# Query turning moved two projections back, router judging moved later, and one layernorm's statistics moved into the stage before it, in a one-core transformer kernel on Trainium2

## Chip, core and metric

The kernel runs on one core of a Trainium2 chip. The metric is device time in microseconds of one execution. The kernel before was timed three times: 2847.12 us in the median, 2845.57 to 2850.18. TensorE (PE in the profile) multiplies and transposes, VectorE (DVE) and ScalarE (ACT) do elementwise work and reductions, GpSimd (POOL) does elementwise work between on-chip tiles, SyncE (SP) issues transfers. Each engine works through its own queue in order and waits on semaphores that others raise.

## The reference

One sequence of 2048 tokens of width 256 goes through four residual blocks. Each begins with a layernorm.

```python
x = x + attn_a(layernorm(x), ...)   # 16 heads, low-rank keys and values, a mask of top-k index scores
x = x + ffn(layernorm(x), ...)      # 8 routed experts, 2 per token, and a shared one
x = x + attn_b(layernorm(x), ...)   # 16 heads of 16, ALiBi
x = x + ffn(layernorm(x), ...)      # the same weights again
```

The parts that the change touches:

```python
def layernorm(x): m = mean(x); v = var(x); return (x - m) / sqrt(v + 1e-5)

# attn_a: the index mask
index_scores = einsum('bhqk,h->bqk', relu(qi @ ki), idx_w)     # 2048 x 2048
thr = sorted_desc(index_scores)[adaptive_k - 1]                # one threshold per row
mask = where(index_scores >= thr, 0, -1e9), with the causal mask
# attn_a: its queries
q = (x @ Wq).reshape(b, s, 16, 128 + 64); rope on the last 64
scores = q_full @ k_full * scale + mask

# ffn: the router
scores = softmax(xf @ gate_w); sel = top_k(scores + expert_bias, 2)
out = shared(xf); out[token] += routed expert of the token
```

## The kernel before

The 2048 rows are 16 tiles of 128 (`NT`), `x` stays on chip, and `xT` holds the normalized rows transposed. Every stage is a block in which each engine has a queue written out by hand. Between blocks all engines meet at a barrier, so a block's end is its last engine's end. There is no scheduler: the order in the code is the order in the queue.

**Index threshold** (`index_threshold`, called twice, once for each half of the mask's rows; `g` is 0 or 1, `ixt0` and `ixt1` in semaphore names). VectorE and ScalarE search the k-th largest score of each row. Five probes (`PROBES`) each try a midpoint: VectorE counts the scores above it in four of eight row tiles (L784), ScalarE in the other four with a sign and a sum (L629), then VectorE narrows the bounds with some twenty small operations and publishes the next midpoint (`mid_ready`, L724), at last `hi_ready` (L806). A step over eight row tiles follows: ScalarE writes marks above `hi` (L637, L642), VectorE masks and takes the top eight (L810, L813). Then VectorE writes the mask `bias` (L730, L736). The first threshold writes the short rows of the causal triangle, the second the long ones.

Beside the search runs a second job, eight heads' queries for 16 row tiles, "pairs" `n` = 0 to 15, since each has two halves of four heads:

- TensorE projects pair `n` (L664) into two of four PSUM banks and raises `projected`.
- ScalarE copies it to `q_nat[n % 3]` (L590, `store_projected`) and raises `q_ready`.
- GpSimd applies the rope to the pair in place (L571 to L575), behind a given midpoint, and raises `roped`.
- TensorE turns the pair, eight transposes (L674), into two PSUM banks that all pairs share, once the pair before has been copied from them (`q_taken`), and raises `flipped`.
- ScalarE copies the turned pair to `q_out` (L600, `store_flipped`) and raises `q_taken`; SyncE stores it to HBM (L552).

ScalarE's order is a list of units: copies of projections 0 and 1, then alternately projection `n + 2` and turned pair `n`. Three units stand after each probe's signs, one after every second row tile of the step above `hi`, the rest at the end. TensorE's order is projection `n`, turning `n - 1`. Behind all pairs stands a small matmul (L678), for which VectorE waits with `ix_unsolved` (L834); then the block ends.

**Layernorm** (`layernorm`, four times). VectorE takes statistics of 16 tiles (`bn_stats`, L137), computes mean and variance, ScalarE the square root, VectorE normalizes tile by tile (L158), TensorE transposes (L206), ScalarE stores to `xT` (L173). The second and fourth also compute the router's logits: for each quarter `n` of the rows `judge(n)` multiplies `gate_w` by `xT` (L189), `keep_verdict(n)` on ScalarE copies the result (L167), `turn_verdict(n)` transposes it on TensorE (L197).

**Experts** (`experts`, twice). At its end VectorE adds the two routed results of each quarter of the rows to `x` (L2316, L2318), as the quarter's transfers land. The first call is followed by the third layernorm.

## Time and profile before

| what | value |
|---|---|
| median of three runs | 2847.12 us |
| the profiled execution | 2841.48 us |
| its span, first to last instruction | 2839.6 us |
| TensorE matmul busy | 2335.7 us, 82% of the span |
| VectorE busy | 1783.8 us, 63% |
| ScalarE busy | 1678.7 us, 59% |
| GpSimd busy | 704.2 us, 25% |
| mean granted TensorE clock | 0.908 |

The profile is of one execution. Its busy shares are averages over stages, and each stage here has another limit. A wait is read from the idle time before an instruction and from what released it. The first index threshold lies at 169 to 359 us, the second at 462 to 653, the four layernorms end near 24, 1784, 2007 and 2628. The granted clock of a stretch is a share of 2.4 GHz: 0.5 is the lower of TensorE's two levels, 1.2 GHz, and values between are stretches with both.

### The profile page before, as it was taken

Reading aid. Unit: us, or ns where it says so; the run is one execution under the profiler, and the core shown is the slowest. Engines: PE = TensorE matmul, PEld = TensorE weight load, DVE = VectorE, ACT = ScalarE, POOL = GpSimd, SP = SyncE. Lnnn points to the kernel's source line nnn. Section 1 sums busy time; section 2 is a strip of 40 time slices with the busy share of each in tenths; the row PEclk is TensorE's granted clock in tenths of the full one; section 3 lists DMA queues with packets and bytes.
Section 4 is the critical chain, followed back from the end, with each engine's and each line's share of the span. In section 5 each row is a group of like instructions: output and inputs, shape, how many; then the busy total and the mean of one; then the engine's idle time right before and its main releaser. Section 6 shows DMA issues by size and latency. Waiting matters only on the chain. (4 is left out here: it accounts for less than half of the span.)

```text
span 2839.6 us, 42530 instructions
## 1 busy us (share of the span) xinstructions
PE 2335.7 (82%) x12560; PEld 1566.7 (55%) x12561; DVE 1783.8 (63%) x3726; ACT 1678.7 (59%) x3051; POOL 704.2 (25%) x974
## 2 busy tenths in 40 slices
PE   4954585556999999999999997986639999997985
PEld 2532253225877787877777885554315444434653
DVE  4786669673777677767776776523347778823523
ACT  2776667673877777777777765232306777763232
POOL 0213420342422332133225322154010000000153
PEclk9977897787999999999999998998858999977998
DMA  1011101014100000000001001223360303000124
GB/s 47 0 38 45 53 22 37 37 52 136 31 16 12 21 21 15 12 24 16 16 8 31 8 1 59 77 78 115 132 99 1 46 2 46 2 1 3 53 80 135
DMA packets 78250, 115.62 MB, mean 41 GB/s; under 512 B 24658, under 2 KB 52146, under 8 KB 75058
## 3 DMA queue, kind: packets, MB, share of 16 engines
q1 hardware_dynamic: 67796, 91.62, 11.6%
q0 software_dynamic: 10240, 21.38, 2.5%
q8 instruction: 105, 1.72, 0.2%
q14 instruction: 109, 0.89, 0.1%
HBM read 70.63 MB, written 41.94 MB: 40 GB/s over the span
## 5 line engine op out<-in xcount | busy, mean ns | idle before, releaser
L1389 DVE TENSOR_TENSOR aa_pt_lo<-psum,aa_pt_hi 128x512 fp32r<-128x512 f32 x544 | 350.5, 686 | 82.6 <-ACT aa_pt_hi L1319 80.0
L1840 DVE TENSOR_REDUCE ab_part_max<-psum 128x2 f32<-128x1024 f32 (+3 forms) x320 | 327.3, 1062 | 116.4 <-PE psum L1678 114.4
L1782 ACT ACTIVATE ab_prob<-psum 128x512 f32<-128x512 f32 (+3 forms) x640 | 298.0, 542 | 121.2 <-PE psum L1707 117.1
L1319 ACT ACTIVATE aa_pt_hi<-psum 128x512 fp32r<-128x512 f32 x544 | 297.4, 598 | 116.2 <-PE psum L1249 113.3
L1376 DVE CUSTOM_DVE_ANT_0 aa_prob<-psum,bias 128x512 f32<-128x512 f32 (+2 forms) x480 | 278.7, 598 | 113.2 <-PE psum L1239 93.9
L1237 PE MATMUL psum<-ka_hi,aa_q_hi 128*128 128x512 f32 (+3 forms) x640 | 267.9, 419 | 11.1 <-POOL aa_q_lo L1171 8.3
L1203 POOL TENSOR_TENSOR x<-aa_y_out,x 128x256 f32<-128x256 f32 x256 | 188.2, 735 | 353.4 <-ACT aa_y_out L1337 308.7
L1249 PE MATMUL psum<-ident,aa_prob 128*128 128x128 f32 x1600 | 253.0, 274 | 6.8 <-issue 5.5
L1707 PE MATMUL psum<-ab_q_stack,ab_k_stack 50*128 50x512 f32 (+3 forms) x640 | 243.7, 460 | 13.2 <-ACT ab_prob L1782 8.8
L1311 ACT ACTIVATE aa_prob<-aa_prob,aa_neg_max 128x128 f32<-128x128 f32 (+11 forms) x192 | 228.0, 1188 | 43.8 <-DVE aa_neg_max L1382 42.0
L1260 PE MATMUL psum<-aa_pt_hi,c_stack 128*128 128x512 f32 x544 | 233.6, 429 | 5.9 <-ACT aa_out_t L1326 4.3
L1238 PE MATMUL psum<-ka_lo,aa_q_hi 128*128 128x512 f32 (+3 forms) x640 | 235.8, 368 | 2.0 <-issue 2.0
L1239 PE MATMUL psum<-ka_hi,aa_q_lo 128*128 128x512 f32 (+3 forms) x640 | 236.3, 369 | 0.0
L1678 PE MATMUL psum<-ab_k_stack,ab_q_stack 49*128 49x512 f32 (+3 forms) x640 | 230.4, 475 | 6.3 <-DVE ab_part_max L1840 6.0
L1262 PE MATMUL psum<-aa_pt_lo,c_stack 128*64 128x512 f32 x544 | 215.5, 396 | 0.0
L1249 PEld LDWEIGHTS psum<-ident,aa_prob 128*128 128x128 f32 x1600 | 193.7, 141 | 30.3 <-issue 8.3
L1707 PEld LDWEIGHTS psum<-ab_q_stack,ab_k_stack 50*128 50x128 f32 x640 | 119.2, 203 | 116.7 <-ACT ab_prob L1782 84.9
L674 PE MATMUL psum<-ident,ixt_q_nat 128*128 128x128 f32 x256 | 46.7, 342 | 148.6 <-ACT ixt_q_out L600 141.6
L1171 POOL TENSOR_TENSOR aa_q_lo<-aa_q_row,aa_q_hi 128x512 fp32r<-128x512 f32 x64 | 82.4, 1289 | 333.1 <-ACT aa_q_hi L1303 333.1
L1719 PE MATMUL psum<-ab_prob,values 128*17 128x512 f32 (+3 forms) x1280 | 163.2, 585 | 0.0
L664 PE MATMUL psum<-ixt_w_heads,xT 128*128 128x512 f32 x256 | 141.2, 704 | 22.4 <-ACT ixt_w_heads L583 22.4
L2161 DVE SCALAR_TENSOR_TENSOR f_h<-psum,f_found,f_silu 128x224 f32<-128x224 f32 x80 | 36.1, 451 | 188.1 <-ACT f_silu L2129 188.1
(334 smaller groups left out, 4922.8 us busy)
## 6 DMA issues: line engine op xcount, KB each, us to landing
q_rows<-ixt_q_out SPq DMA_DIRECT2D x64, 256.0 KB, 2.1
aa_q_row<-q_rows SPq DMA_DIRECT2D x64, 256.0 KB, 2.6
f_back<-done SPq DMA_DIRECT2D x16, 512.0 KB, 7.6
w<-in_w SPq DMA_DIRECT2D x6, 896.0 KB, 11.3
x<-in_hidden SPq DMA_DIRECT2D x2, 2048.0 KB, 11.5
ab_q_stack<-stash_q_hi SPq DMA_DIRECT2D x32, 128.0 KB, 10.4
ab_k_stack<-stash_k_hi SPq DMA_DIRECT2D x32, 128.0 KB, 11.9
ixt_wq_n<-in_Wq_nope_T SPq DMA_DIRECT2D x2, 1024.0 KB, 5.6
```

Source lines behind the costliest of these rows:

```text
L1237: nc.tensor.matmul(out[:, 0:w], q_hi[t % 2][:, head], k_hi[:, cols], start=True, stop=False)
L1238: nc.tensor.matmul(out[:, 0:w], q_hi[t % 2][:, head], k_lo[:, cols], start=False, stop=False)
L1239: nc.tensor.matmul(out[:, 0:w], q_lo[t % 2][:, head], k_hi[:, cols], start=False, stop=True).then_inc(scores_ready, 1)
L1249: last = nc.tensor.transpose(turn_bank[(TB[t] + j) % RING][:, h * P:(h + 1) * P], prob[t % 2][h][:, j * P:(j + 1) * P], const["ident"][:])
L1260: nc.tensor.matmul(out[:], c_stack[:, j, :], pt_hi[ring][:], start=j == 0, stop=j == t, skip_group_check=True)
L1319: nc.scalar.activation(pt_hi[(TB[t] + j) % RING][:], turn_bank[(TB[t] + j) % RING], ACT.Copy).then_inc(pt_hi_done, 1)
L1376: nc.vector.tensor_tensor_reduce(prob[t % 2][h][:, c * CH:c * CH + w], score_bank[(QB[t] + h * chunks[t] + c) % 2][:, 0:w], bias[:, TRI[t] ...
L1389: nc.vector.tensor_tensor(pt_lo[ring][:], turn_bank[(TB[t] + j) % RING], pt_hi[ring][:].bitcast(F32), ALU.subtract).then_inc(pt_lo_done, 1)
L1678: nc.tensor.matmul(out[:, 0:w], q[at, t * P:(t + 1) * P], k[at, part * CH:part * CH + w], start=not diag, stop=True, skip_group_check=True ...
L1707: nc.tensor.matmul(out[:, 0:w], k[at, kb * P:(kb + 1) * P], q[at, q0:q0 + w], start=not diag, stop=True, skip_group_check=True).then_inc(t ...
L1782: nc.scalar.activation(prob[i % 2][h][:, 0:w], t_bank[slot % RING][:, 0:w], ACT.Exp).then_inc(t_taken, 1)
L1840: nc.vector.tensor_reduce(part_max[e % 2][:, at:at + 5:4, part], s_pair[pair % 2][:, :, 0:w], AX.X, ALU.max).then_inc(s_used, 1)
```

## The change

1. On TensorE in the index threshold the turning of pair `n` stands behind projection `n + 2` instead of `n + 1`. ScalarE's and GpSimd's orders stay.
2. In the second and fourth layernorm `judge(n)` moves three transposed tiles back, from tile 4(n+1) to tile 4(n+1)+3, and `turn_verdict(n)` from there to behind `judge(n + 1)`. ScalarE's `keep_verdict(n)` moves four tiles back.
3. The first `experts` takes the third layernorm's statistics: four `bn_stats` behind each quarter's additions, into a tile `stats` that `program` now allocates. The third layernorm gets them and leaves its own out.

```diff
-                    if logits is not None and t >= 5 and t % 4 == 1:
-                        keep_verdict(t // 4 - 1)
+                    if logits is not None and t >= 9 and t % 4 == 1:
+                        keep_verdict(t // 4 - 2)
                 if logits is not None:
+                    keep_verdict(NCH - 2)
                     keep_verdict(NCH - 1)
...
-                    if logits is not None and t >= 4 and t % 4 == 0:
+                    if logits is not None and t >= 7 and t % 4 == 3:
                         judge(t // 4 - 1)
-                    if logits is not None and t >= 4 and t % 4 == 3:
-                        turn_verdict(t // 4 - 1)
+                        if t >= 11:
+                            turn_verdict(t // 4 - 2)
                 if logits is not None:
                     judge(NCH - 1)
+                    turn_verdict(NCH - 2)
                     turn_verdict(NCH - 1)
...
-                for n in range(PAIRS + 1):
+                for n in range(PAIRS + 2):
...
-                    if n >= 1:
-                        pe.wait_ge(roped, n)
-                        if n >= 2:
-                            pe.wait_ge(q_taken, 2 * (n - 1))
+                    if n >= 2:
+                        pe.wait_ge(roped, n - 1)
+                        if n >= 3:
+                            pe.wait_ge(q_taken, 2 * (n - 2))
                         for i in range(2):
                             for h in range(GH):
                                 last = nc.tensor.transpose(flip_bank[i][:, h * P:(h + 1) * P],
-                                                           q_nat[(n - 1) % RING][:, i * GH + h, :], const["ident"][:])
+                                                           q_nat[(n - 2) % RING][:, i * GH + h, :], const["ident"][:])
...
                     nc.vector.tensor_tensor(here, here, back[n][1][:], ALU.add).then_inc(added, 1)
+                    if stats is not None:
+                        dve.wait_ge(added, n + 1)
+                        for t in range(n * CHUNK, (n + 1) * CHUNK):
+                            nc.vector.bn_stats(stats[:, t, :], x[:, t, :])
...
+        stats = sb("stats", [P, NT, 6])
...
-            experts(nc, "f1", x, xT, xn, bank, const, router, w13, w2, shared_in, routed_in, rows, done)
-        layernorm(nc, "ln3", x, xT, bank, const["ident"], mean, rstd)
+            experts(nc, "f1", x, xT, xn, bank, const, router, w13, w2, shared_in, routed_in, rows, done, stats=stats)
+        layernorm(nc, "ln3", x, xT, bank, const["ident"], mean, rstd, stats=stats)
```

TensorE's queue in the first index threshold, before, from the turning of pair 0 on (`ixt_q_nat_1375` to `_1377` are the three tiles of the ring, `ixt_w_heads` the projection's weights):

```order
L674 MATMUL psum<-ident,ixt_q_nat_1375 128x128 [waits ixt0_roped]
L674 MATMUL psum<-ident,ixt_q_nat_1375 128x128 x7
L664 MATMUL psum<-ixt_w_heads,xT 128x512 [waits ixt0_q_ready]
L664 MATMUL psum<-ixt_w_heads,xT 128x512 x3
L674 MATMUL psum<-ident,ixt_q_nat_1376 128x128 [waits ixt0_q_taken,ixt0_roped]
L674 MATMUL psum<-ident,ixt_q_nat_1376 128x128 x7
L664 MATMUL psum<-ixt_w_heads,xT 128x512 [waits ixt0_q_ready]
L664 MATMUL psum<-ixt_w_heads,xT 128x512 x3
```

The same place of the changed kernel, from projection 2 on:

```order
L669 MATMUL psum<-ixt_w_heads,xT 128x512 [waits ixt0_q_ready]
L669 MATMUL psum<-ixt_w_heads,xT 128x512 x3
L679 MATMUL psum<-ident,ixt_q_nat_1375 128x128 [waits ixt0_roped]
L679 MATMUL psum<-ident,ixt_q_nat_1375 128x128 x7
L669 MATMUL psum<-ixt_w_heads,xT 128x512 [waits ixt0_q_ready]
L669 MATMUL psum<-ixt_w_heads,xT 128x512 x3
L679 MATMUL psum<-ident,ixt_q_nat_1376 128x128 [waits ixt0_q_taken,ixt0_roped]
L679 MATMUL psum<-ident,ixt_q_nat_1376 128x128 x7
```

Projection 3, the second of the projections in either piece, stood behind the turning of pair 1 with its wait for `q_taken`, and now stands ahead of it.

TensorE's queue in the second layernorm, before (`xn_first` are normalized tiles, two transposes each; `f_gate_w` is a judgement, `ln_verdict` a verdict's turning):

```order
L206 MATMUL psum<-ident,xn_first 128x128 x10
L189 MATMUL psum<-xT,f_gate_w 8x512 x2
L206 MATMUL psum<-ident,xn_first 128x128 x6
L197 MATMUL psum<-ident,ln_verdict 128x8 x4
L206 MATMUL psum<-ident,xn_first 128x128 x2
```

And now:

```order
L210 MATMUL psum<-ident,xn_first 128x128 x16
L193 MATMUL psum<-xT,f_gate_w 8x512 x2
L210 MATMUL psum<-ident,xn_first 128x128 x8
L193 MATMUL psum<-xT,f_gate_w 8x512 x2
L201 MATMUL psum<-ident,ln_verdict 128x8 x4
```

The first verdict's turning stood three tiles behind its judgement, and now stands four tiles and the next judgement behind it.

VectorE's queue at the end of the first experts, now, for one quarter (`f_back` are the routed results; before, the additions of the quarters stood next to each other):

```order
L2321 TENSOR_TENSOR x<-x,f_back 128x1024 [waits ln1_stats_done]
L2323 TENSOR_TENSOR x<-x,f_back 128x1024 [waits ixs0_staged]
L2327 BN_STATS stats<-x 128x6 [waits ixs0_cleared]
L2327 BN_STATS stats<-x 128x6 x3
L2321 TENSOR_TENSOR x<-x,f_back 128x1024 [waits ixp_dve_step]
```

Four of the sixteen statistics lie between the additions of two quarters. (Semaphores are reused by later stages under their first name.)

## Rows read from the trace of the kernel before

**Rows 1.** Waits, first threshold: engine line, waited for: us, times, longest

```profile
PE psum L674 <- ACT ixt_q_out L600: 70.8, 14, 10.6
ACT ixt_q_nat L590 <- PE psum L664: 55.4, 22, 5.6
```

**Rows 2.** Waits, second index threshold

```profile
ACT ixt_q_nat L590 <- PE psum L664: 56.1, 22, 5.6
```

**Rows 3.** Timeline, ScalarE: start, us, engine line op [idle before]

```profile
211.90 1.06 ACT L590 ACTIVATE ixt_q_nat<-psum 128x512 f32<-128x512 f32 x2
...
219.22 0.60 ACT L590 ACTIVATE ixt_q_nat<-psum 128x512 f32<-128x512 f32 x1 [5.29 <-PE psum L664]
...
221.38 1.99 ACT L629 ACTIVATE x<-ix_scores,ix_neg_mid 128x2048 bf16<-128x2048 f32 x1
...
229.75 1.06 ACT L600 ACTIVATE ixt_q_out<-psum 128x512 f32<-128x512 f32 x2
...
292.38 1.99 ACT L637 ACTIVATE x<-ix_scores,ix_neg_hi 128x2048 bf16<-128x2048 f32 x1
```

**Rows 4.** Timeline, TensorE, after the first probe's signs

```profile
214.08 1.94 PE L674 MATMUL psum<-ident,ixt_q_nat 128*128 128x128 f32 x8 [5.18 <-ACT ixt_q_out L600]
215.81 5.03 PE L664 MATMUL psum<-ixt_w_heads,xT 128*128 128x512 f32 x8
```

**Rows 5.** Timeline, VectorE, first to second probe

```profile
212.03 0.17 DVE L787 TENSOR_SCALAR ix_count<-ix_signs 128x4 f32<-128x4 f32 x1 [5.66 <-ACT x L629]
...
215.34 2.35 DVE L784 TENSOR_SCALAR_CACHE_REDUCE bias<-ix_scores,ix_mid 128x2048 bf16<-128x2048 f32 x1 [0.38 <-DVE ix_neg_mid L724]
```

**Rows 6.** Windows (us, PE/PEld/DVE/ACT/POOL busy, PEclk, DMA, GB/s); timelines, tail

```profile
214.00:231.00 17.00, 6.81 (x17) 3.76 (x18) 10.92 (x21) 10.43 (x12) 7.79 (x8) 0.70 0.08 31
328.00:359.00 31.00, 20.28 (x82) 11.06 (x82) 18.88 (x31) 11.93 (x23) 22.62 (x20) 0.99 0.26 101
...
335.72 1.07 PE L674 MATMUL psum<-ident,ixt_q_nat 128*128 128x128 f32 x8 [1.76 <-ACT ixt_q_out L600]
336.62 3.60 PE L664 MATMUL psum<-ixt_w_heads,xT 128*128 128x512 f32 x8
...
357.47 1.09 PE L674 MATMUL psum<-ident,ixt_q_nat 128*128 128x128 f32 x8 [1.91 <-POOL ixt_q_nat L575]
...
344.51 1.60 POOL L575 TENSOR_TENSOR ixt_q_nat<-ixt_straight,ixt_crossed 128x512 f32<-128x512 f32 x1
...
353.45 1.26 POOL L571 TENSOR_TENSOR ixt_straight<-ixt_q_nat,ixt_rope 128x512 f32<-128x512 f32 x1 [2.28 <-ACT ixt_q_nat L590]
```

**Rows 7.** Timelines, ScalarE and VectorE, end of the first threshold

```profile
327.28 1.06 ACT L590 ACTIVATE ixt_q_nat<-psum 128x512 f32<-128x512 f32 x2
...
345.02 2.12 DVE L736 TENSOR_TENSOR bias<-bias,causal 128x128 bf16<-128x128 bf16 x8
358.79 0.16 DVE L834 TENSOR_SCALAR ix_unsolved<-psum 128x1 int32<-128x1 f32 x1 [11.65 <-PE psum L678]
```

**Rows 8.** Timelines, ScalarE and VectorE, end of the second threshold

```profile
620.81 1.06 ACT L590 ACTIVATE ixt_q_nat<-psum 128x512 f32<-128x512 f32 x2
...
633.03 12.25 DVE L730 TENSOR_SCALAR bias<-ix_scores,ix_thr 128x1152 bf16<-128x1152 f32 x8
645.31 4.81 DVE L736 TENSOR_TENSOR bias<-bias,causal 128x128 bf16<-128x128 bf16 x8
653.06 0.16 DVE L834 TENSOR_SCALAR ix_unsolved<-psum 128x1 int32<-128x1 f32 x1 [2.93 <-PE psum L678]
```

**Rows 9.** Waits and timeline, TensorE, second layernorm

```profile
PE psum L197 <- ACT ln_verdict L167: 2.2, 4, 0.7
...
1784.09 0.41 PE L197 MATMUL psum<-ident,ln_verdict 8*128 8x8 f32 x4 [0.68 <-ACT ln_verdict L167]
```

**Rows 10.** Timeline, VectorE, first experts' end and third layernorm

```profile
1981.42 1.23 DVE L2316 TENSOR_TENSOR x<-x,f_back 128x1024 f32<-128x1024 f32 x1 [0.53 <-DMA f_back<-done]
...
1993.27 5.32 DVE L137 BATCH_NORM_STATS2 ln_stats<-x  x16 [3.44 <-PEq L91]
```

More of the change, by code:

```diff
@@ L96, in __exit__, with layernorm @@
         return super().__exit__(kind, *rest)
-def layernorm(nc, tag, x, xT, bank, ident, mean, rstd, keep=None, gate_w=None, gate_in=None, logits=None, load=None):
+def layernorm(nc, tag, x, xT, bank, ident, mean, rstd, keep=None, gate_w=None, gate_in=None, logits=None, load=None, stats=None):
     DEEP = 4
@@ L103, in layernorm @@
         sb, sem = phase.sb, phase.sem
-        stats = sb("stats", [P, NT, 6])
+        known = stats is not None
+        if not known:
+            stats = sb("stats", [P, NT, 6])
         half = sb("half", [P, NT])
@@ L133, in _ @@
             def _(dve):
-                with dve.Fori(0, NT // DEEP) as i:
-                    for p in range(DEEP):
-                        at = bass.ds(i * DEEP + p, 1)
-                        nc.vector.bn_stats(stats[:, at, :], x[:, at, :]).then_inc(stats_done, 1)
-                dve.wait_ge(stats_done, NT)
+                if not known:
+                    with dve.Fori(0, NT // DEEP) as i:
+                        for p in range(DEEP):
+                            at = bass.ds(i * DEEP + p, 1)
+                            nc.vector.bn_stats(stats[:, at, :], x[:, at, :]).then_inc(stats_done, 1)
+                    dve.wait_ge(stats_done, NT)
                 chain = Chain(dve, dve_step)
@@ L1867, in _, with experts @@
                                                 inv[p][:].to_broadcast([P, HB, DHB]), ALU.mult).then_inc(o_done, 1)
-def experts(nc, tag, x, xT, xn, bank, const, router, w13, w2, shared_in, routed_in, rows, done, store=None):
+def experts(nc, tag, x, xT, xn, bank, const, router, w13, w2, shared_in, routed_in, rows, done, store=None, stats=None):
     gate_w, prior, before, number, lane, code, trash = (router[name] for name in (
@@ L2365, in program @@
             attention_a(nc, arg, x, xT, bank, const, k_hi, k_lo, c_stack, bias, w_out, nowhere, q_rows)
+        stats = sb("stats", [P, NT, 6])
         w13 = sb("w13", [P, KC, EE, 2 * HID])
```

## The prediction

> **What bounds the kernel now.** I began with the waits of the first index threshold, because the change touches it most. TensorE waits 70.8 us there for ScalarE's copies of turned queries (`ixt_q_out`), and ScalarE waits 55.4 us for the projections of TensorE [rows 1]; the second threshold repeats it with 56.1 us [rows 2]. Two engines that wait for each other in turn mean that the order of TensorE's queue is the bound. The timelines show how. ScalarE copies projection 2 at 211.90 and the turned queries 0 right behind; the copy of projection 3 then waits 5.29 us [rows 3]. On TensorE projection 3 stands behind the turning of queries 1, which may not start until the turned queries 0 are copied: it starts at 214.08 after 5.18 us of idling, and the projection follows at 215.81 [rows 4]. All that time TensorE could have projected. The next probe's signs can start only at 221.38, after it. VectorE is no bound: it idles 5.66 us for the signs, computes the next midpoint, and counts from 215.34 on [rows 5]. So one phase (a probe's signs and three query units on ScalarE) takes (292.38 - 221.38) / 4 = 17.75 us, from the second probe to the step above `hi`.
>
> After the last phase the same cycle runs without signs: TensorE waits 1.76 us in each pair [rows 6], and the end of this stage is set by its queue: `ix_unsolved` waits until 358.79 (11.65 us) for the last matmul in the first threshold, and until 653.06, but only 2.93 us, in the second, where VectorE's write of the mask takes 12.25 + 4.81 us [rows 7, 8].
>
> **The query turning, first threshold.** With the new order projection 3 stands ahead of turning 1 and needs only copy 1, so it is ready while the signs run. From 211.90: copies of projection 2, turned 0 and projection 3 are about 1.05 us each (two of 0.5), done at 215.1, where the midpoint is there too. Then each phase is the longer of two chains. VectorE: four counts of 2.27 us (2.35 with the overlap, [rows 5]) and 3.3 us of small operations (212.03 to 215.34), 12.4 us. ScalarE: 8.4 us of signs (221.38 to 229.75, [rows 3]) and 3.2 us of copies, 11.6 us; in every other phase two turned pairs are to be copied, and the second turning cannot start before the first is copied: 1.94 us of turning at the lower clock [rows 4] beside a 1.06 us copy of a projection, so 1 us more: 12.6. I take 12.5 for three phases and 11.8 for the last, where the step to `hi` has fewer small operations. Start of the step above `hi`: 215.1 + 37.5 + 11.8 = 264.4 instead of 292.38, **28.0 us** less. I followed GpSimd too: each rope waits for a midpoint that is there by then, and ends 4.0 us later (353.45 to 357.47, [rows 6]), well ahead of its turning; the ring of three `q_nat` never blocks, since turning n-3 stands ahead of projection n on TensorE.
>
> The step above `hi` stays at its length, as its signs and VectorE's masked maxima set it: 292.38 to 327.28 [rows 3, 7], so now 264.4 to 299.3. The tail on TensorE then, by rows: the copies of projection 11 and turned 9 until 301.4; turning 10 and projection 13 at the lower clock, 1.9 + 5.0 [rows 4]; turning 11, projection 14, turning 12, projection 15, turning 13 at the higher clock, 0.9 + 3.6 + 0.9 + 3.6 + 0.9 [rows 6], until 318.4. Now GpSimd is the late one: rope 14 starts at 314.0 and takes some 5.2 us instead of 4.0, an estimate: beside the mask's write an operation took 1.60 us that takes 1.26 elsewhere [rows 6]. Rope 15 is done at 323.4, turning 15 at 324.6, the verdict at 325.2. That is against 358.79: **33.6 us**. Today the tail is 31.5 us from 327.28, then it is 25.9. VectorE's write ended at 347.1 (345.02 + 2.12, [rows 7]) and moves to 319.1, so it is not last, by 6 us.
>
> **Second threshold.** The phases give the same 28.0 us. The tail differs: the write starts 12.2 us after the copy at 620.81, as in the first (633.03), and takes 17.1 us [rows 8] beside the ropes, so VectorE ends at 650.1 - 28 = 622.1 at most. The ropes beside it are slower in turn: I take 6 us each for rope 14 and rope 15, half again as long as alone (an estimate, since here `L736` too is slowed more than in the first threshold, [rows 7, 8]), and they end near 620, the last matmul near 621.3. Both chains end together; I take 621.7, **31.4 us** less than 653.06. The Trainium skill (SBUF — State Buffer, SBUF: two separate sides) says that VectorE in a two-port mode or with two SBUF inputs and GpSimd lock each other out for a whole instruction. This trace agrees in kind: the eight `L736` operations take 2.12 us in the first threshold and 4.81 in the second [rows 7, 8]. By the rule alone a denser tail could cost more; as no more ropes than today's three can lie beside the write, I count nothing above its present length.
>
> **Router's judging, second and fourth layernorm.** TensorE waits four times, 2.2 us in all, for a copied verdict, 0.7 of it at the end [rows 9]. Three of the waits go, 1.5 us: each verdict's turning now stands four transposes and another judgement behind its copy. The last wait (0.68 us before the row at 1784.09) stays, but one turning of 0.41 us moves into it. That is 1.9 us each, 3.8 for both. Bounds: 0, if ScalarE's copies, which now bunch at the end, hold the judging; 2.5 if the first judgement also runs at the higher clock.
>
> **Third layernorm.** Its statistics (5.32 us, [rows 10]) go from the start of the layernorm to behind each quarter of the additions. The additions wait for transfers of 0.53 us and about the same before the third and fourth quarter, 1.5 us together, so 1.5 of the 5.3 us are hidden and 3.8 are not; four short waits on the second addition cost 0.1 each. Net 5.3 - 4.2 = **1.1 us**. Bounds: -0.5 (statistics hidden nowhere, waits dearer) and 3 (the loop's entry goes too).
>
> **Sum.** 33.6 + 31.4 + 3.8 + 1.1 = 69.9 us. The profiled execution took 2841.5 us and would take 2771.6; the median of the runs shown, 2847.1, is 5.6 us above it, and gives **2777 us**. Uncertain is mainly TensorE's clock in the phases, and how VectorE and GpSimd delay each other: 2 to 3 us per threshold either way, so 2768 to 2786 for this case alone.
>
> **Rivals.**
> A. TensorE's queue is the bound at a mixed clock. It ran at 0.70 of full speed in a phase and at 0.99 in the tail [rows 6]. After the change it still idles about once in two phases. If projections cost 5 us and turnings 1.9 throughout, also in the tail, a pair costs 6.9 us: a phase needs 1.5 pairs, 10.4 us, and stays hidden behind 12.4, but the tail loses 2 x 1.4 + 3 x 1.0 us more, and the phases about 1 us each through the turnings. That is 11 us per threshold less gain: 2799 us. For it: the granted clock. Against it: the tail's 0.99 with pauses of 1.76 us.
> B. Lower clock throughout, and slower than before. A pair then costs 2 x 3.6 + 1.94 = 9.1 us, and 1.5 pairs 13.7 us, above VectorE's 12.4: from that point (8.3 us a pair) TensorE decides. From 214.08 on [rows 4] fifteen turnings and twelve projections are 29.1 + 86.4 = 115.5 us, some 25 us are lost where a turning waits for ScalarE to finish its signs (5 us in each of five phases), and rope 15 with its turning hangs behind at 6 us: 361 us, 2 us later than now. The last two turnings, which now stand together behind the last projection, each wait for a copy, some 1.8 us [rows 6]. So some 5 us later in each threshold: 2847 + 10 - 5 = 2852 us. The Trainium skill (TensorE: Matmul & The Clock Gate, HAM oscillation) warns of just such bursts with pauses between them. The trace agrees that pauses cost the clock (5.03 us against 3.6 for a projection), but it also shows the clock rise within one burst, which this rival denies.
> C. The change does not reach what sets the phases: ScalarE's wait only moves from the projection to the turned queries, at 3 us (1.94 of turning, 1.06 of copying) in each of ten phases. Against it: turning n is preceded by nothing unfinished except projection n+2. Gain 40 us: 2807 us.
>
> **Chances.** The forecast 0.77; A 0.12; C 0.07; B 0.04. The range that holds 8 in 10 is 2764 to 2796: below the forecast by a rest of the bounds (layernorms, and a clock that stays high in the phases), above it by most of A. What a measurement of this kernel can tell from no change is 0.2%, 6 us. Faster by more than that: forecast, A and C, 0.96; no change 0.02 and slower 0.02 share B.
>
> **What would show it.** Right: in the changed profile ScalarE's copies of projections follow each other with no 5 us wait, the signs start every 12.4 to 12.6 us, `ix_count` waits under 1 us, the verdict comes 33 and 31 us earlier counted from each threshold's start, and the second is released by GpSimd's or VectorE's work rather than by copies. TensorE shows no waits of 0.5 us for `ln_verdict` inside the layernorms. `BATCH_NORM_STATS2` lies four at a time between the additions. Wrong: phases above 13 us with TensorE busy, which is A or B; waits of ScalarE for `psum` by the turnings, which is C; a mask write longer than 17 us.

## The result and the profile after

The changed kernel takes 2780.32 us in the median of four runs (2772.26 to 2787.32), the kernel before 2846.35 beside it: ratio 0.9765, 95% interval 0.9741 to 0.9789. It is faster by 66.0 us; forecast were 69.9, and 2777 us. Measured again on another chip (five runs, below) it took 2775.21 against 2847.16: 0.975, interval 0.9729 to 0.977. The profiled execution took 2778.29 us, its span is 2776.4.

The waits of the first threshold, changed kernel, TensorE, ScalarE and VectorE (engine line, waited for: us, times, longest). They answer to [rows 1]; lines of the thresholds have moved by five.

```profile
PE psum L679 <- ACT ixt_q_out L605: 39.2, 8, 11.7
ACT ixt_q_nat L595 <- PE psum L669: 15.6, 10, 3.9
ACT ixt_q_out L605 <- PE psum L679: 7.6, 6, 4.1
DVE ix_count L792 <- ACT x L634: 5.8, 1, 5.8
```

TensorE still waits for the copies of turned pairs, but no projection stands behind that wait. ScalarE's wait for projections falls from 55.4 to 15.6 us, of which 7.9 lie ahead of the first signs and the rest behind the step above `hi`: within the phases none is left. The wait that could have taken its place, for turned pairs, is 7.6, and all but 0.6 of it lies behind the step too. VectorE waited for ScalarE's signs five times before, 26.5 us, and now waits once, in the first probe.

ScalarE's timeline there (start, us, engine line op, [idle before]), against [rows 3]: the second to fifth probe and the step above `hi`.

```profile
212.97 1.06 ACT L595 ACTIVATE ixt_q_nat<-psum 128x512 f32<-128x512 f32 x2
213.92 1.08 ACT L605 ACTIVATE ixt_q_out<-psum 128x512 f32<-128x512 f32 x2
214.87 1.10 ACT L595 ACTIVATE ixt_q_nat<-psum 128x512 f32<-128x512 f32 x2
216.06 2.00 ACT L634 ACTIVATE x<-ix_scores,ix_neg_mid 128x2048 bf16<-128x2048 f32 x1
...
228.43 2.00 ACT L634 ACTIVATE x<-ix_scores,ix_neg_mid 128x2048 bf16<-128x2048 f32 x1 [0.98 <-DVE ix_neg_mid L729]
...
240.75 2.00 ACT L634 ACTIVATE x<-ix_scores,ix_neg_mid 128x2048 bf16<-128x2048 f32 x1 [0.93 <-DVE ix_neg_mid L729]
...
251.47 0.60 ACT L605 ACTIVATE ixt_q_out<-psum 128x512 f32<-128x512 f32 x1 [0.29 <-PE psum L679]
252.32 0.60 ACT L605 ACTIVATE ixt_q_out<-psum 128x512 f32<-128x512 f32 x1 [0.26 <-PE psum L679]
253.07 2.00 ACT L634 ACTIVATE x<-ix_scores,ix_neg_mid 128x2048 bf16<-128x2048 f32 x1 [0.16 <-DVE ix_neg_mid L729]
...
264.32 2.04 ACT L642 ACTIVATE x<-ix_scores,ix_neg_hi 128x2048 bf16<-128x2048 f32 x1
```

The three copies are back to back. Phases start 12.37, 12.32 and 12.32 us apart, and ScalarE now waits for VectorE's midpoint, up to 0.98 us, while VectorE waits for no signs: VectorE is the bound. The step above `hi` starts at 264.32 where 264.4 was forecast, but the first signs stand 1.06 us later in this profile (204.59, before 203.53). Counted from them the step comes after 59.7 us, 1.1 less than forecast and 29.1 less than before.

The tail is where it came out otherwise. VectorE's write of the mask (two loops of eight operations; those of the first loop grow from one tile of 128 columns to eight, and a merged line shows the shape of the first) and the small matmul's reader, first threshold. The first line is of the kernel before, whose others are in [rows 7]:

```profile
339.51 5.48 DVE L730 TENSOR_SCALAR bias<-ix_scores,ix_thr 128x128 bf16<-128x128 f32 x8
...
312.68 9.04 DVE L735 TENSOR_SCALAR bias<-ix_scores,ix_thr 128x128 bf16<-128x128 f32 x8
321.75 3.19 DVE L741 TENSOR_TENSOR bias<-bias,causal 128x128 bf16<-128x128 bf16 x8
326.66 0.16 DVE L839 TENSOR_SCALAR ix_unsolved<-psum 128x1 int32<-128x1 f32 x1 [1.73 <-PE psum L683]
```

And in the second, against [rows 8]:

```profile
572.00 13.65 DVE L735 TENSOR_SCALAR bias<-ix_scores,ix_thr 128x1152 bf16<-128x1152 f32 x8
585.69 2.64 DVE L741 TENSOR_TENSOR bias<-bias,causal 128x128 bf16<-128x128 bf16 x8
589.93 0.16 DVE L839 TENSOR_SCALAR ix_unsolved<-psum 128x1 int32<-128x1 f32 x1 [1.59 <-PE psum L683]
```

The first write takes 12.26 us (312.68 to 321.75 + 3.19), not the 7.6 of before (339.51 to 345.02 + 2.12); the second 16.33, not 17.09. GpSimd's timeline says what lies beside the first: the end of rope 13, rope 14 (four operations from 314.94 on) and rope 15, of which the first operation is shown:

```profile
313.38 1.39 POOL L580 TENSOR_TENSOR ixt_q_nat<-ixt_straight,ixt_crossed 128x512 f32<-128x512 f32 x1
314.94 1.27 POOL L576 TENSOR_TENSOR ixt_straight<-ixt_q_nat,ixt_rope 128x512 f32<-128x512 f32 x1 [0.17 <-POOL ixt_q_nat L580]
316.16 0.92 POOL L577 TENSOR_TENSOR ixt_crossed<-ixt_q_nat,ixt_rope 128x256 f32<-128x256 f32 x1
317.05 0.97 POOL L578 TENSOR_TENSOR ixt_crossed<-ixt_q_nat,ixt_rope 128x256 f32<-128x256 f32 x1
318.09 1.46 POOL L580 TENSOR_TENSOR ixt_q_nat<-ixt_straight,ixt_crossed 128x512 f32<-128x512 f32 x1
319.72 1.45 POOL L576 TENSOR_TENSOR ixt_straight<-ixt_q_nat,ixt_rope 128x512 f32<-128x512 f32 x1 [0.17 <-POOL ixt_q_nat L580]
```

and TensorE's what follows them, the turnings of pairs 14 and 15:

```profile
319.60 1.09 PE L679 MATMUL psum<-ident,ixt_q_nat 128*128 128x128 f32 x8 [2.47 <-POOL ixt_q_nat L580]
324.37 1.97 PE L679 MATMUL psum<-ident,ixt_q_nat 128*128 128x128 f32 x8 [3.67 <-POOL ixt_q_nat L580]
```

The ropes of pairs 11 to 15 now run back to back, 0.17 us apart, and the last sets the end, as forecast; the last turning, after 3.67 us of idle, runs at the lower clock. Counted from the first probe's signs, the first threshold takes 122.07 us instead of 155.26, the second 125.97 instead of 156.33: **33.2 and 30.4 us**.

The second layernorm on TensorE, from the first transpose to the experts' first matmul. Before (see [rows 9] for the waits):

```profile
1765.80 2.39 PE L206 MATMUL psum<-ident,xn_first 128*128 128x128 f32 x10 [12.78 <-DVE xn_first L158]
1768.33 3.56 PE L189 MATMUL psum<-xT,f_gate_w 128*8 128x512 f32 x4
...
1786.53 3.25 PE L2058 MATMUL psum<-w,xT 128*128 128x448 f32 x8 [2.02 <-DVEq L2204]
```

And now:

```profile
1705.05 3.45 PE L210 MATMUL psum<-ident,xn_first 128*128 128x128 f32 x16 [12.78 <-DVE xn_first L161]
1708.44 1.88 PE L193 MATMUL psum<-xT,f_gate_w 128*8 128x512 f32 x4
...
1719.17 0.41 PE L201 MATMUL psum<-ident,ln_verdict 8*128 8x8 f32 x4 [0.34 <-ACT ln_verdict L170]
1721.60 3.14 PE L2063 MATMUL psum<-w,xT 128*128 128x448 f32 x4 [2.02 <-DVEq L2209]
```

This stage takes 16.5 us instead of 20.7, the fourth layernorm's 17.4 instead of 20.4: 7.2 us, 3.8 forecast. VectorE at the end of the first experts, with [rows 10] before:

```profile
1917.77 1.41 DVE L2327 BATCH_NORM_STATS2 stats<-x 128x6 f32<-128x256 f32 x4
1919.09 1.21 DVE L2321 TENSOR_TENSOR x<-x,f_back 128x1024 f32<-128x1024 f32 x1
```

Four statistics stand between additions, and the addition behind them waits for no transfer. From the first addition to the third layernorm's first transpose it is 20.6 us instead of 22.4: 1.8, 1.1 forecast.

Together the stages give 33.2 + 30.4 + 7.2 + 1.8 us, unrounded 72.5, between these two profiles, and the profiled executions differ by 63.2. Stretches whose code did not change lost the other 9.3: attention A's 2.4, attention B's 1.7, the two experts up to their additions 1.8 and 3.0, and 1.1 ahead of the first signs, less 0.6 between the thresholds. Other profiles, below, say whether the change does that.

### The profile page after: what moved, and what is told of

Read it like the earlier page. It is cut to its first block and busy times, and to the rows that moved or that the text cites. A ratio compares the mean times of both kernels' runs of the same rounds, so it can differ in the third digit from the quotient of the medians.

```text
span 2776.4 us, 42489 instructions
## 1 busy us (share of the span) xinstructions
PE 2332.4 (84%) x12560; PEld 1566.9 (56%) x12561; DVE 1789.3 (64%) x3726; ACT 1678.2 (60%) x3051; POOL 709.6 (26%) x974
## 5 line engine op out<-in xcount | busy, mean ns | idle before, releaser
L1242 PEld LDWEIGHTS psum<-ka_hi,aa_q_hi 128*128 128x128 f32 x640 | 123.4, 193 | 48.5 <-DVE aa_chunk_max L1381 17.6
```

Of the source, the lines that this page charges most:

```text
L1242: nc.tensor.matmul(out[:, 0:w], q_hi[t % 2][:, head], k_hi[:, cols], start=True, stop=False)
```

## Experiments

The first four ran on one chip, the next four on another, the last two together. Durations of stages are from the profiles, one execution each; "the changed kernel" beside them is that of the section above, thresholds 122.07 and 125.97 us. Of the kernel without the last ropes and of the last two there is one execution, so no interval.

**Each part alone.** The turning of pair `n` behind projection `n + 2`, everything else as before (diffs here are against the changed kernel; the layernorms' orders go back likewise):

```diff
-            experts(nc, "f1", ..., done, stats=stats)
-        layernorm(nc, "ln3", ..., mean, rstd, stats=stats)
+            experts(nc, "f1", ..., done)
+        layernorm(nc, "ln3", ..., mean, rstd)
...
```

> The kernel before with part 1 alone: TensorE turns pair n behind projection n + 2. Theory (the two thresholds carry the gain, 33.2 and 30.4 us in the changed profile): 62 to 66 us less than before, ratio 0.977 to 0.979, phases of 12.3 to 12.4 us, tail as in the changed kernel; the layernorms as before. Rival (the parts help each other, for instance through TensorE's clock): under 58 us less.

Measured: ratio 0.9733 (0.9678 to 0.9787), 2775.74 us against 2849.2. The thresholds take 122.05 and 125.98 us; the two layernorm stages 19.9 us each, the statistics' stage 23.0 (one of the three transfer waits there is 1.12 us instead of 0.53). Its experts take 195.2 and 195.5 us. The thresholds give the forecast 63.6 us. The whole kernel took 73.5 less, outside the theory's 62 to 66, while the ratio's interval reaches into its range. Two of its four executions (2757.13 and 2770.33 us) ran at a mean granted clock of 0.921 and 0.918, the other two at 0.909 and 0.912; the last section tells where such executions gain.

The norms' parts with the old turning:

```diff
-                for n in range(PAIRS + 2):
+                for n in range(PAIRS + 1):
...
-                    if n >= 2:
-                        pe.wait_ge(roped, n - 1)
+                    if n >= 1:
+                        pe.wait_ge(roped, n - 0)
...
```

> The changed kernel with the turning put back one projection behind: parts 2 and 3 alone. Theory: the second and fourth layernorm 4.2 and 3.0 us shorter up to the first expert matmul, as in the changed profile, and 1.1 us at the third, of which some is lost where the experts start at the lower clock; 3 to 8 us less in all, ratio 0.997 to 0.999. Rival (the layernorm's gain is given back in the experts): within 2 us of before.

Measured: ratio 0.9969 (0.9955 to 0.9984). The thresholds take 155.47 and 156.33 us, as before; the layernorm stages 17.0 and 17.0, the statistics' stage 20.6. The median is 8.5 us lower. So by stages the gain is the sum of separate parts, 63.6 us by the turning and 8 to 9 by the rest; the medians of so few executions do not add up as well. The experts take 193.4 to 195.9 us in every profile but that of the kernel before (191.9 and 192.3), in these two as well, each of which lacks what the other has. That neither edit alone is needed for it is shown; why the one profile of before is quicker there stays open.

**Turning one projection later still**, behind projection `n + 3`:

```diff
-                for n in range(PAIRS + 2):
+                for n in range(PAIRS + 3):
...
-                                                           q_nat[(n - 2) % RING][:, i * GH + h, :], const["ident"][:])
+                                                           q_nat[(n - 3) % RING][:, i * GH + h, :], const["ident"][:])
```

> The changed kernel with pair n turned behind projection n + 3. Theory (one step took the copy out of the projections' way, and the phases are now set by VectorE's counts and small operations, 12.3 us): phases unchanged, the tail within 3 us, since one more turning hangs behind the last projection but GpSimd's ropes set its end; total within 6 us of the changed kernel. Rival (distance itself pays): 10 us or more less.

Measured: ratio 0.9717 (0.9663 to 0.977), 2774.94 us, the thresholds 122.04 and 126.00 us, each phase as in the changed kernel. Turning later still changes neither phases nor tail. That TensorE does not bound the phases, at either clock, follows from VectorE's waits above: after the first probe it waits for no signs, in this kernel's equal phases too.

**The last three ropes left out** (pairs 13 to 15 are turned without rope; that part of the work is missing):

```diff
+                    if n >= 13:
+                        pool.sem_inc(roped, 1)
+                        continue
```

> The changed kernel without the rope of pairs 13, 14 and 15 in either threshold: GpSimd only raises the semaphore. Theory (GpSimd's ropes and VectorE's write of the mask slow each other): the write of the mask takes 4 us less in the first threshold (12.3 to about 8) and 5 us less in the second (16.3 to about 11), and TensorE's last turning no longer waits 3.7 and 5.4 us for a rope; the stage then ends with VectorE, 4 to 6 us earlier each. Rival (the write is slow for another reason, and only the ropes' own length matters): the write keeps its length, the stage ends where the write ends now, under 2 us earlier.

Measured: 2761.19 us; 116.58 and 116.59 us for the thresholds, 5.5 and 9.4 less (4 to 6 expected). VectorE's write in the first one is (timeline; lines moved by three more):

```profile
310.88 3.53 DVE L738 TENSOR_SCALAR bias<-ix_scores,ix_thr 128x128 bf16<-128x128 f32 x8
314.44 1.17 DVE L744 TENSOR_TENSOR bias<-bias,causal 128x128 bf16<-128x128 bf16 x8
320.73 0.16 DVE L842 TENSOR_SCALAR ix_unsolved<-psum 128x1 int32<-128x1 f32 x1 [5.12 <-PE psum L686]
```

Beside no rope the write takes 4.73 us, against 12.26; in the second threshold 8.99 against 16.33. The ropes cost VectorE 7.5 and 7.3 us, more than the 4 and 5 expected, and the rival, a write that keeps its length, is refuted. The theory missed the end: neither threshold ends with VectorE here. The last turnings wait for ScalarE's copies, and the verdict comes 5.12 us behind the first write and 0.88 behind the second. In the changed kernel too the last turning ends both thresholds, behind GpSimd's last rope, and the write ends only 1.7 and 1.6 us ahead of the verdict. So both chains would have to shorten, GpSimd's and VectorE's, and ropes done earlier can do both.

**The work moved out of the tail.** Three kernels do that, with the changed one beside them.

> The changed kernel once more, as the measure for the three kernels that share its chip. Both theories: the ratio to the kernel before as measured, 0.973 to 0.979; both thresholds as in its first profile, 122.1 and 126.0 us from the first probe's signs to the verdict, the mask writes 12.3 and 16.3 us.

Measured: 2775.21 us, ratio 0.975; thresholds 122.02 and 125.99 us, writes 12.25 and 16.33, as expected.

Two copies instead of one behind every second row tile of the step above `hi`:

```diff
-                        queries(3 * PROBES + 2 + j // 2, 3 * PROBES + 3 + j // 2)
-                queries(3 * PROBES + 2 + GT // 2, 2 * PAIRS)
+                        queries(3 * PROBES + 2 + 2 * (j // 2), 3 * PROBES + 2 + 2 * (j // 2 + 1))
+                queries(3 * PROBES + 2 + 2 * (GT // 2), 2 * PAIRS)
```

> The changed kernel with two of ScalarE's copies instead of one behind every second row tile of the step above hi. Theory (the copies, ropes and turnings that lie beside and behind the step cost more at the end than inside it; there VectorE sets the pace with some 4.7 us a row tile, and ScalarE has up to 0.6 us a tile to spare): the step keeps its length within 1 us, seven copies instead of eleven follow it, fewer ropes lie beside the mask write, which shrinks to 5 to 9 us in the first threshold and 9 to 13 in the second; the verdicts come 3 to 5 and 5 to 9 us earlier, the kernel is 8 to 13 us faster than the changed one. Rival (ScalarE has nothing to spare in the step): the step grows by 4 us, four copies of 1.06, the verdicts come 0 to 1 us earlier, and the kernel is within 3 us of the changed one.

Measured: 2770.05 us, ratio 0.9729 (0.9706 to 0.9753), an interval that overlaps the changed kernel's. The thresholds take 118.54 and 122.45 us, 3.5 less each. From the step's start to the write it is 46.55 us instead of 48.33, so ScalarE had the room. But the write takes 10.66 and 14.87 us, not 5 to 9 and 9 to 13: two ropes still lie beside it. The kernel is 5.2 us below the changed one, not 8 to 13. The mechanism held, its size was forecast too large.

Four copies instead of three behind each probe's signs:

```diff
-                    scan = max(0, (2 * n - 4) // 3 + 1)
+                    scan = max(0, (2 * n - 4) // 4 + 1)
...
-                    queries(3 * r + 2, 3 * r + 5)
+                    queries(4 * r + 2, 4 * r + 6)
...
```

The first pair of lines lets each rope wait for the midpoint of the phase in which its copy now stands; the lists of copies in and behind the step are renumbered to match.

> The changed kernel with four of ScalarE's copies instead of three behind each probe's signs. Theory: a phase now costs ScalarE 8.4 us of signs and 4.2 of copies, 12.7, against 12.3 on VectorE, so four phases grow by 0.4 to 1 us each and the step above hi starts 1.5 to 4 us later; six copies instead of eleven follow the step, the mask writes shrink as in the kernel with two copies in the step, and the verdicts come 1 to 3 and 4 to 7 us earlier: 5 to 9 us faster than the changed kernel. Rival (each fourth copy waits for a turning that itself waits for the copy before, 2 us more a phase): the step above hi starts 7 to 8 us later, the verdicts 3 us later to 1 us earlier, and the kernel is 0 to 6 us slower.

Measured: 2763.22 us, ratio 0.9709 (0.9692 to 0.9727). Phases take 12.19, 13.09, 12.99, 12.35 and 12.19 us, so the step above `hi` starts 3.1 us later, in the theory's range. The write takes 4.72 and 9.00 us, as short as without the late ropes, and the thresholds 116.32 and 120.55, 5.7 and 5.4 less: the first gains more than the 1 to 3 us expected. The kernel is 12.0 us below the changed one, 5 to 9 expected. In two of the five phases ScalarE now waits for a turning, but 0.3 us twice (timeline of this kernel), not the 2 us of the rival:

```profile
230.30 0.60 ACT L605 ACTIVATE ixt_q_out<-psum 128x512 f32<-128x512 f32 x1 [0.29 <-PE psum L679]
231.16 0.60 ACT L605 ACTIVATE ixt_q_out<-psum 128x512 f32<-128x512 f32 x1 [0.26 <-PE psum L679]
231.65 1.99 ACT L634 ACTIVATE x<-ix_scores,ix_neg_mid 128x2048 bf16<-128x2048 f32 x1
```

Both together, so that two copies are left for the tail:

```diff
-                    scan = max(0, (2 * n - 4) // 3 + 1)
+                    scan = max(0, (2 * n - 4) // 4 + 1)
...
-                    queries(3 * r + 2, 3 * r + 5)
+                    queries(4 * r + 2, 4 * r + 6)
...
-                        queries(3 * PROBES + 2 + j // 2, 3 * PROBES + 3 + j // 2)
-                queries(3 * PROBES + 2 + GT // 2, 2 * PAIRS)
+                        queries(4 * PROBES + 2 + 2 * (j // 2), 4 * PROBES + 2 + 2 * (j // 2 + 1))
+                queries(4 * PROBES + 2 + 2 * (GT // 2), 2 * PAIRS)
```

> Four copies behind each probe's signs and two behind every second row tile of the step above hi, so only two follow it. Theory: the phases cost 1.5 to 4 us as with four copies alone, the mask write has no rope beside it in either threshold (4.7 and 9 us, as without the last three ropes), and the small matmul ends no later than the write; 6 to 12 us faster than the changed kernel, no more than 3 us from the better of the two single edits. Rival (ScalarE's copies set the step and the phases): both grow by 4 us, and the kernel is within 3 us of the changed one.

Measured: **2753.34 us**, ratio 0.9688 (0.9665 to 0.9711), the lowest median here; its interval overlaps that of four copies alone. The thresholds take 114.23 and 118.52 us, 7.8 and 7.5 less than the changed kernel's. VectorE's timeline at the end of the first:

```profile
314.04 3.52 DVE L735 TENSOR_SCALAR bias<-ix_scores,ix_thr 128x128 bf16<-128x128 f32 x8
317.60 1.17 DVE L741 TENSOR_TENSOR bias<-bias,causal 128x128 bf16<-128x128 bf16 x8
318.80 0.16 DVE L839 TENSOR_SCALAR ix_unsolved<-psum 128x1 int32<-128x1 f32 x1
```

No wait is left before the reader of the small matmul: the block ends with VectorE's own work, as it does with four copies alone. Phases of up to 13.1 us show that ScalarE sets some of them now. The medians differ by 21.9 us from the changed kernel's and by 9.9 from that with four copies, more than the 6 to 12 and 3 that the theory allowed. The thresholds account for 15.3 and 4.1 of it, itself above the theory; the rest lies in stages that the edit does not touch (the last section says what varies there).

**The judgements back at their place**, the verdicts' turnings late:

```diff
-                    if logits is not None and t >= 7 and t % 4 == 3:
+                    if logits is not None and t >= 4 and t % 4 == 0:
                         judge(t // 4 - 1)
-                        if t >= 11:
-                            turn_verdict(t // 4 - 2)
+                    if logits is not None and t >= 11 and t % 4 == 3:
+                        turn_verdict(t // 4 - 2)
```

> The changed kernel with the judgements back at their old place (behind the transposes of tile 4(n+1)), the verdicts' turnings and the copies staying late. Read is the stage from the second and fourth layernorm's first transpose to the experts' first matmul, 20.2 us on average before and 17.0 changed. Theory (half of the 3.2 us is the first judgement, which ran at the lower clock, 3.56 us against 1.88, since it came earlier in the burst of transposes; the other half the waits for copied verdicts): 18.4 to 18.9 us. Rival (all of it is the waits, and the clock rises where it rises wherever the judgement stands): 16.8 to 17.3 us.

Measured: 20.1 and 19.9 us (2783.60 in all). Both theories missed: all of the gain is gone, not half or none. TensorE's timeline in the second layernorm of this kernel:

```profile
1704.67 2.40 PE L210 MATMUL psum<-ident,xn_first 128*128 128x128 f32 x10 [12.79 <-DVE xn_first L161]
1707.20 3.57 PE L193 MATMUL psum<-xT,f_gate_w 128*8 128x512 f32 x4
1710.70 1.12 PE L210 MATMUL psum<-ident,xn_first 128*128 128x128 f32 x8
1712.20 1.88 PE L193 MATMUL psum<-xT,f_gate_w 128*8 128x512 f32 x4 [0.37 <-ACT xT L176]
1714.01 0.87 PE L210 MATMUL psum<-ident,xn_first 128*128 128x128 f32 x6
1715.39 0.41 PE L201 MATMUL psum<-ident,ln_verdict 8*128 8x8 f32 x4 [0.50 <-ACT ln_verdict L170]
```

The first judgement is back at the lower clock, 3.57 us against 1.88 (3.31 against 2.54 in the fourth layernorm). But the waits for copied verdicts are back too, 0.50 us twice, with a new one of 0.37 for `xT`, although the turnings stand as late as in the changed kernel. ScalarE copies `xT` tiles and verdicts in one queue, and here the verdict's copy still stands late in it, behind the copy of tile 9. What covered it in the changed kernel was the next judgement ahead of the turning, 1.88 us of work; the turning's later place, with the copy later as well, covers nothing. The waits are 1.4 us more than in the changed kernel (1.71 against 0.34), the first judgement 1.7 and 0.8.

**The statistics behind all additions**, instead of four behind each quarter:

```diff
-                    if stats is not None:
-                        dve.wait_ge(added, n + 1)
-                        for t in range(n * CHUNK, (n + 1) * CHUNK):
-                            nc.vector.bn_stats(stats[:, t, :], x[:, t, :])
+                if stats is not None:
+                    dve.wait_ge(added, NT // CHUNK)
+                    for t in range(NT):
+                        nc.vector.bn_stats(stats[:, t, :], x[:, t, :])
```

> The changed kernel with all sixteen statistics of the third layernorm behind the last quarter's additions, still in the experts' block. Read is the stage from the first addition to the third layernorm's first transpose, 22.4 to 22.9 us before and 20.6 changed. Theory (the statistics between the additions lie in the wait for the next quarter's transfer): the waits of some 0.5 us before the second to fourth quarter come back and the stage takes 21.9 to 22.3 us. Rival (the gain is that of the left-out loop and its wait in the layernorm): 20.5 to 20.9 us.

Measured: 22.1 us, the theory's figure (2781.64 in all). VectorE's timeline:

```profile
1918.74 1.23 DVE L2321 TENSOR_TENSOR x<-x,f_back 128x1024 f32<-128x1024 f32 x1 [0.54 <-DMA f_back<-done]
...
1927.23 5.32 DVE L2327 BATCH_NORM_STATS2 stats<-x 128x6 f32<-128x256 f32 x16
```

Of the gain, 1.4 to 1.5 us is the three waits of about half a microsecond; the other 0.4 goes with the layernorm's own loop (0.9 against the kernel with the turning alone, where one transfer wait was 0.6 us longer). The first experts, up to the first addition, take 195.3 us here and 195.2 with the turning alone, and 193.4 to 193.7 in every kernel that has the statistics between the additions; the kernel before, without them, had 191.9, so what this follows is not shown.

## Why the prediction was right, step by step

| step | forecast, us | measured, us |
|---|---|---|
| first threshold | 33.6 | 33.2 |
| second threshold | 31.4 | 30.4 |
| judging, both layernorms | 3.8 | 7.2 |
| third layernorm's statistics | 1.1 | 1.8 |
| sum | 69.9 | 72.5 |
| whole kernel, medians | 69.9 | 66.0 and 71.9 |

- **What set the phases** was read rightly: ScalarE's wait for a projection held behind a turning. It went with the order alone, the other parts left out, and was there again with the old order. Rival C, the wait merely moving, did not occur: in the phases 0.6 us of waits for turned pairs are left. A and B, projections at 5 us or turnings at 1.9 throughout, did not either: from the second projection of the tail on TensorE's rows are 3.60 and 1.04 us, and only the last turning is slow.
- **The phases' length** was forecast as 12.5 us with ScalarE the longer of the two in every other phase (12.6). Measured is VectorE's 12.3, in three, and 11.25 for the last (11.8 forecast). The extra microsecond for a second turned pair was too much: in one such phase, with the turning at 1.06 us, there is no wait for it and ScalarE has 0.98 to spare; in the other, with the turning at 1.94, the waits are 0.29 and 0.26 us and 0.16 is to spare.
- **"VectorE's write ... moves to 319.1, so it is not last, by 6 us"** failed. It ended at 324.94, 1.7 us ahead of the verdict. The prediction gave it the length of before, 7.6 us, although the same paragraph had put two ropes beside it. That did no harm because the write was not on the chain, and the ropes were sized well: 9.4 us for ropes 14 and 15 together, forecast and measured. The tail came out 62.3 us instead of 60.8 from the step above `hi`: rope 14 starts 1.0 us later behind the step, and the last turning runs at the lower clock. That the threshold's 33.2 us lie so near 33.6 is partly luck: the phases saved 1.1 us more than forecast, the tail 1.5 less.
- **The second threshold** has both chains ending within 2 us of each other, as forecast; the write was no longer than before, 16.3 against 17.1. The missing microsecond is again the difference of two misses. The phases saved 29.5 us, not 28.0. The tail saved 0.9, not 3.4: rope 14 starts 0.8 us later than two ropes of 6 us that end near 620 would, the last two ropes take 13.0 us instead of 12, and from the last rope to the verdict it is 2.4 instead of 1.7, since the last turning runs at the lower clock.
- **The judging** was sized at 1.9 us a layernorm and gives 4.2 and 3.0. The waits came as forecast: three of 0.50 us gone, the last down from 0.68 to 0.34, 1.8 us. The term that was put at nothing in the sum, and at 0.6 in the bound, is the first judgement's clock: 3.56 and 3.25 us before, 1.88 and 2.54 after, since sixteen transposes stand ahead of it instead of ten; another 0.7 and 0.4 are not placed. This pair of profiles is a favourable one. With the old order (the kernel before, the turning alone) the stage takes 19.9 to 20.7 us and the first judgement 2.70 to 3.56; with the new one, in nine kernels, 16.4 to 17.9 and 1.88 to 3.01. On the average the stage gains 3.0 us and the judgement 0.7, so both layernorms together are worth some 6 us rather than 7.2.
- **The statistics**: the hidden transfers (1.5) were right, the loop's entry (bound 3, "the loop's entry goes too") goes in part, 0.4 us.
- **The total.** The prediction had no term for stages that it leaves alone, and they took 9.3 us between these profiles. The stages' surplus over the forecast, 2.6 us, covers a part of that; the whole is off by 4 us in the medians of the first chip and by 2 in those of the second.

The Trainium skill (SBUF — State Buffer, SBUF: two separate sides) calls the port pair that VectorE and GpSimd share an exclusive lock: while a VectorE instruction in a two-port mode or with two SBUF inputs, or a GpSimd one, holds it, the other engine fully blocks for the whole instruction. By their lengths undisturbed, the write (4.7 us) and GpSimd's work beside it (some 9.9, from 312.68 on) would then take 14.6 us one after the other; the trace shows 12.3. Direction and most of the size agree, an exclusion of whole instructions, end to end, does not; in which mode the write's operations ran, and which part of them overlapped, no run here shows.

## What to carry to other kernels

Where a queue holds a wait that is satisfied late, look at what stands behind it and needs nothing late: moving that work ahead of the wait took 29 us per call ahead of the step above `hi` (88.9 to 59.7 us from the first signs) at no cost to the phases, once the waits of its consumer had been followed through. A wait is covered by work placed between producer and consumer, not by a later place for both. And when an edit pulls a tail forward, measure again what now lies side by side: here ropes beside it made a write 7.5 us longer, and copies moved forward on ScalarE took that back and brought the last rope forward with it, 7.8 and 7.5 us of a threshold. And read a term in more than one profile: the thresholds repeat within 0.2 us in this case, the judging stage only within 1.5.

## What was not expected of the hardware

**Who pays for sharing.** VectorE's first loop of the mask write, eight operations with one f32 tensor operand, took 3.52 us alone and 9.04 beside ropes, while a rope of 4.0 us took 4.6 beside it. In the second threshold both paid: the write 7.3 us, ropes 14 and 15 some 2.4 and 2.5 us each. Small ones suffer as well: in the changed kernel an operation of 0.16 us took 1.13 there (`ix_bad` by `ix_outside`, 310.82), and 0.16 in the kernel with four and two.

**The clock within a busy stretch.** The last 110 us of attention B, code that no kernel here changes, run at a granted clock of 0.65 in the kernel before, 0.67 in the changed one, and 0.94 in two other executions. Windows (us, PE, PEld, DVE, ACT and POOL busy, PEclk, DMA, GB/s) of before, the changed kernel, the norms' parts alone:

```profile
2499.00:2609.00 110.00, 94.37 (x465) 41.28 (x461) 29.82 (x81) 50.86 (x111) 1.99 (x4) 0.65 0.01 3
```

```profile
2435.00:2546.00 111.00, 95.12 (x471) 41.26 (x469) 31.00 (x83) 51.91 (x114) 1.99 (x4) 0.67 0.01 2
2455.00:2520.00 65.00, 60.48 (x237) 20.13 (x231) 3.79 (x13) 30.26 (x65) 0.00 (x0) 0.50 0.00 1
```

```profile
2476.00:2586.00 110.00, 89.95 (x630) 43.91 (x626) 47.92 (x99) 65.97 (x145) 1.99 (x4) 0.94 0.02 3
```

TensorE was busy 60.5 of 65 us at half clock, so no pause explains it. In the 10 us across which the clock falls (2445 to 2455) it was busy 9.1. The stage from the third to the fourth layernorm takes 603 to 612 us with the low stretch and 584.6 or 587.9 without. The two executions without it are the shortest of their kernels, 2817.43 us of the norms' parts alone and 2737.49 of the kernel with four and two; their mean granted clock was 0.915 and 0.921, that of the others of these kernels 0.904 to 0.911. Executions of other kernels that were as short for theirs (2823.84, 2757.13, 2750.16) had 0.916 to 0.921, but were not profiled. That is some 20 us between executions of one kernel, whose thresholds repeat within 0.2 us; why it occurs in some executions only stays open. It is why the terms above are read from stages and not from totals.
